# A regrouped conv result moved to every fourth partition instead of to 32 neighbouring ones

## The reference, cut to what matters

```python
# layer 0: a grouped conv, 4 groups of 16 channels, 9 taps, padding 4
out = conv(x, L0_weight, groups=4)                  # [128, 64, 1024]
x = x + out + (cond_128 @ L0_c_weight.T)[:, :, None] + fside_S_0[None, :, None]
# layers 1, 2, 3: a 1x1 conv whose 64x64 weight is mixed per sample from 8
h = gelu(gelu(cond_128 @ W0 + b0) @ W1 + b1)
att = softmax(h @ W2 + b2)                          # [128, 8]
x = x + einsum('boi,bih->boh', einsum('bk,koi->boi', att, weight), x) + (att @ bias_k)[:, :, None]
```

## Time and profile before

| what | value |
|---|---|
| median of 3 runs | 383.65 us (382.25 to 386.31) |
| span of the profiled execution, first to last instruction | 383.4 us |
| PE busy | 336.6 us, 88% of the span |
| DVE busy | 282.8 us, 74% |
| ACT busy | 242.8 us, 63% |
| POOL busy | 122.4 us, 32% |
| packets of the one DMA queue in use | 94.4% of 16 engines' span |
| TensorE clock granted, mean | 0.985 |

### The profile page before, as it was taken

One profiled execution on the slowest core, in us unless ns is written; L12 is line 12 of the kernel. 1 busy time (PEld: TensorE's weight loads), 2 busy tenths in 40 slices (PEclk: granted clock), 3 DMA queues, 4 the chain that ended last, 5 costly groups with the idle time before them and its releaser, 6 DMA issues.

```text
span 383.4 us, 6039 instructions
## 1 busy us (share of the span) xinstructions
PE 336.6 (88%) x1542; PEld 271.4 (71%) x1542; DVE 282.8 (74%) x298; ACT 242.8 (63%) x415; POOL 122.4 (32%) x172
## 2 busy tenths in 40 slices
PE   6404998799988999999999999999999999899955
PEld 5103877578867877777877887877777877777843
DVE  5711699688777877787888888877788777788463
ACT  3503597977665666666666666666666666666553
POOL 9000401234411344444444444444444311124000
PEclk9999998799999999999999999999999999999997
DMA  7896099399999999999999999999999999998985
GB/s 254 152 129 149 0 188 192 109 213 253 277 326 325 314 318 329 331 328 324 328 315 326 327 326 322 323 326 329 322 325 313 285 302 307 315 328 274 220 252 219
DMA packets 28927, 104.43 MB, mean 272 GB/s; under 512 B 3206, under 2 KB 3462, under 8 KB 20855
## 3 DMA queue, kind: packets, MB, share of 16 engines
q1 hardware_dynamic: 28919, 104.34, 94.4%
HBM read 35.89 MB, written 33.55 MB: 181 GB/s over the span
## 4 chain that ended last, share of the span: by engine, by line
PE 37%; DMA 31%; DVE 13%; issue 10%; ACT 5%; SPq 1%; DVEq 1%; ACTq 0%
PE bank L360 20%; DMA mixtab<-conv_sb 20%; DMA mixtab<-out_sb 6%; PE bank L400 5%; PE bank L402 4%; PE bank L401 4%; DMA x_sb<-in_x 4%; DVE mix_f L670 4%; DVE out_sb L684 3%; ACT conv_sb L521 2%; DVE mixtab L663 2%; PE bank L378 2%; DVE mix_lo L675 2%; DMA x_sb<-in_mats 2%; PE bank L455 1%
## 5 line engine op out<-in xcount | busy, mean ns | idle before, releaser
L521 ACT ACTIVATE conv_sb<-bank 128x512 f32<-128x512 f32 x128 | 76.5, 599 | 62.1 <-PE bank L360 58.5
L649 DVE TENSOR_TENSOR x_lo<-x_sb,x_hi 128x2064 fp32r<-128x2064 f32 x31 | 72.6, 2342 | 24.3 <-ACT x_hi L514 24.2
L360 PE MATMUL bank<-x_hi,toep_hi 128*128 128x512 f32 x256 | 86.2, 419 | 2.1 <-ACT conv_sb L521 2.1
L360 PE MATMUL bank<-x_lo,toep_hi 128*128 128x512 f32 x256 | 82.0, 402 | 0.0
L360 PE MATMUL bank<-x_hi,toep_lo 128*128 128x512 f32 x256 | 81.9, 402 | 0.0
L663 DVE TENSOR_TENSOR mixtab<-mixtab 128x2048 fp32r<-128x2048 f32 x31 | 70.7, 2281 | 0.0
L546 ACT ACTIVATE out_sb<-bank,beta 128x512 f32<-128x512 f32 x95 | 65.8, 694 | 5.5 <-PE bank L402 5.4
L400 PE MATMUL bank<-mixtab,mix_hi 128*128 128x512 f32 x128 | 54.6, 427 | 14.3 <-DVE mix_lo L675 10.6
L514 ACT ACTIVATE x_hi<-x_sb 128x2064 fp32r<-128x2064 f32 x32 | 61.6, 1924 | 2.4 <-DMA x_sb<-in_x 2.3
L658 DVE CAST mixtab<-mixtab 128x2048 fp32r<-128x2048 f32 x29 | 35.9, 1239 | 36.3 <-DMA mixtab<-conv_sb 36.0
L301 POOL COPY a_diag<-table 64x128 f32 (+1 forms) x64 | 59.3, 926 | 9.2 <-POOL a_diag L301 4.6
(11 more groups left out here) (77 smaller groups left out, 300.9 us busy)
## 6 DMA issues: line engine op xcount, KB each, us to landing
x_sb<-in_x SPq DMA_DIRECT2D x32, 1032.0 KB, 7.8
mixtab<-conv_sb SPq DMA_DIRECT2D x128, 256.0 KB, 6.3
out<-out_sb SPq DMA_DIRECT2D x31, 1024.0 KB, 8.0
out<-out_sb SPq DMA_DIRECT2D x2, 512.0 KB, 2.6
mixtab<-conv_sb SPq DMA_DIRECT2D x2, 432.0 KB
out_sb<-in_toep SPq DMA_DIRECT2D x1, 640.0 KB, 6.9
x_sb<-in_mats SPq DMA_DIRECT2D x1, 432.0 KB
mixtab<-out_sb SPq DMA_DIRECT2D x1, 432.0 KB
```

The costliest lines, as they stand in the source:

```text
L360: last = mm(o, w[:, d, g, :], v[:, par, g, :, d:d + J], start=i + d == 0, stop=i + d == 3)
L521: nc.scalar.activation(conv_sb[:, par, g, :], conv_ps[g % banks][:, :], ACT.Copy).then_inc(conv_out, 1)
L649: nc.vector.tensor_tensor(x_lo[:, par].rearrange("p g s j -> p (g s j)"), x_sb[:, par].rearrange("p g s j -> p (g s j)"), x_hi[:, par].rea ...
```

## The change

The destination of a move is every fourth partition, `g, g + 4, g + 8, ...`, instead of partitions 32g to 32g + 31. So y's partition order becomes (r, i, g) instead of (g, r, i). What multiplies y must have its rows in that order too: `a21_dup` is laid out (r, i, g), so `a21_copy` reads `pair_ps` with g as its innermost dimension, 16 elements apart, and writes without gaps; the `parity` table is reordered on the host. The number of instructions, DMAs and bytes is the same.

```diff
-        a21_dup = sb("a21_dup", [128, 2, PR, G, 2, CG])
+        a21_dup = sb("a21_dup", [128, 2, PR, 2, CG, G])
@@ move
-                sp.dma_start(y_sb[32 * g:32 * g + 32, par].rearrange("p h s j -> p h (s j)"),
+                sp.dma_start(y_sb[g::G, par].rearrange("p h s j -> p h (s j)"),
                              conv_sb[:, par, g, :]).then_inc(moved[par], 16)
@@ compose_upper
-                              a21_dup[:, par, pr].rearrange("p g r i -> p (g r i)"), a3_diag[:, par, pr, :],
+                              a21_dup[:, par, pr].rearrange("p r i g -> p (r i g)"), a3_diag[:, par, pr, :],
@@ a21_copy
-                    src = pair_ps[:, C * pr:C * pr + C].rearrange("p (g o i) -> p g o i", g=G, o=1)
-                    nc.scalar.activation(a21_dup[:, par, pr], src.to_broadcast([128, G, 2, CG]),
+                    src = pair_ps[:, C * pr:C * pr + C].rearrange("p (o g i) -> p o i g", g=G, o=1)
+                    nc.scalar.activation(a21_dup[:, par, pr], src.to_broadcast([128, 2, CG, G]),
                                          ACT.Copy).then_inc(a21_set, 1)
@@ kernel (host)
-    parity = np.zeros((G, 2, CG, 2), f)
-    parity[:, 0, :, 0] = 1
-    parity[:, 1, :, 1] = 1
+    parity = np.zeros((2, CG, G, 2), f)
+    parity[0, :, :, 0] = 1
+    parity[1, :, :, 1] = 1
```

More of the change, by code:

```diff
@@ L872 @@
         "net": pack(net, NET),
-        "kept": pack({"ident": np.eye(128, dtype=f), "parity": parity}, KEPT),
+        "kept": pack({"ident": np.eye(128, dtype=f), "parity": parity.reshape(128, 2)}, KEPT),
         "row": pack({"frow": a["fside_S_0"], "b2": np.concatenate([a[p + "b2"] for p in mixes])}, ROW),
```

## The result

The changed kernel takes 365.26 us (median of 4 runs, 364.5 to 366.36), the kernel before 384.98 us in the same session (382.25 to 388.42). The ratio is 0.953, with a 95% interval of 0.947 to 0.959: faster. The forecast was 368.0 us, with a range of 361 to 380.

A forecast was written before the change was run, and what follows sets the result against it. The prediction took the loop through the landing of a step's last move to hold steps above PE's pace; 10.8 + 2.3 + 1.0 + 1.5 = 15.6 us off 383.4, plus 0.25, gave 368.0 us, range 361 to 380.

The forecast's parts named there:

- The rate belongs to the destination: Moves: their low rate, 132 GB/s alone, comes from writing 32 neighbouring partitions; every fourth partition spans all 128.
- 390 GB/s for a spread move: Moves: rate taken for the spread destination, between bounds of 132 and 406 GB/s.
- A landing of 3.5 us: Last move of a step: lands about 3.5 us after issue instead of 5.1.
- The loop through the landing: Move, y_high, finish, mix_f, ACT, next move: closes in 9.68 us, bounds steps until the landing is under 4.7 us.
- PE is next: Steady steps: PE's own pace of 9.28 us bounds next, taken as 9.4 us with small gaps.
- The term of 10.8 us for 25 steps: Steady steps: 25 steps fall from 9.83 to 9.40 us each, saving 10.8 us, between 0 and 13.8.
- The start, 2.3 + 1.0 us: Start: ACT's 2.3 us wait for a load goes, and two early steps gain 1 us.
- The end, 1.5 us: End: the last move of step 30 lands earlier, so PE's next mix starts 1.5 us sooner, between 0 and 2.4.
- a21_copy at no cost: ACT's strided PSUM read: change of 0, at most 2 x 0.3 us a step, hidden by ACT's waits.
- (a): Rival for the moves: the rate isn't the destination's, so nothing changes, 383.5 us; chance 0.12.
- (c): Rival for the DMA engines: spread writes collide with the load, making it slower, 399 us or up to 465; chance 0.07.
- (b): Rival for steady steps: partial gain, as single landings still come late or ACT and DVE hold PE, some 376 us; chance 0.08.

The follow-up runs named there:

- e1: Kernel before with only the moves' destination spread to every fourth partition, matrix order not adapted: 366.17 us, ratio 0.951.
- e2: Changed kernel with the moves back to 32 neighbouring partitions, so only the new matrix order remains: 385.93 us, ratio 1.004 to the kernel before.
- e5: Kernel before with moves to every second partition of one 64-partition half, matrix order not adapted: 389.01 us, ratio 1.015.
- e8: Changed kernel without the third product of each mix: 356.77 us, ratio 0.931 to the kernel before.
- e10: Kernel before with ACT doing conv_copy of the last group ahead of mix_high and a finish, no DMA changed: 385.03 us, ratio 1.003.
- e13: Kernel before, moves still slow, storing only two of the four samples of a step: 369.59 us, ratio 0.961.
- e3: Kernel before with spread moves in steps 0 to 2 only, matrix order not adapted: 384.49 us, ratio 1.000.
- e4: Kernel before with spread moves from step 3 on only, matrix order not adapted: 366.87 us, ratio 0.952.
- e9: Changed kernel with the three mixing-table DMAs of the start also writing every fourth partition, result complete: 356.78 us, ratio 0.931 to the kernel before.

## Why the prediction was right, and where not

The forecast of 368.0 us was 2.7 us above the measured 365.26, and its sum of 15.6 us stands against 383.4 - 363.5 = 19.9 us between the two profiled spans.

- *The rate belongs to the destination.* Right, and shown by e1 against e2. The prediction took it that a load or a store differs from a move in just the partitions it touches; they differ in having the device memory at one end too, but e1 changes the partitions alone. The reason given, that the destination spans all 128 partitions, was too simple: by e5 a doubled span has the old rate. Which partitions it touches counts.
- *390 GB/s for a spread move.* About right: 366 GB/s in the window of 48 to 50 us of the changed kernel, and 374 and 381 in that of 50 to 52 of e1 and e8, whose packets are those of moves but for one.
- *A landing of 3.5 us.* Predicted for the last move; 3.5 us is the measured median of all moves, at a share of 0.88 where "under 0.9" was asked for.
- *The loop through the landing closes in 9.68 us and bounds the steps; it stops at 4.7 us.* This is the step of the prediction that failed. The loop is real in the chain, but with it cut (e10) the time stayed, at 1.003 of the kernel before, and the median landing grew from 5.2 to 6.3 us. What held the steps was the time that the DMA queue needs for a step's transfers, which the prediction had beside it ("from 9.8 to 7.9 us, and the queue can drain") and treated as the cause of the latency only. Its sizes for that work are estimates that e13 doesn't bear out as a plain sum. The forecast came out since both readings end at the same next bound, PE; as far as the loop goes, the right time is luck and no evidence for it.
- *PE is next, at 9.28, taken as 9.4.* Right; it was 9.31. The term of 10.8 us for 25 steps was mis-sized by the 0.09 us: from conv_copy of step 5 to that of step 30 the two profiles differ by 13.0 us.
- *The start, 2.3 + 1.0 us.* The profiles differ by 3.8 us between conv_copy of steps 0 and 5 (64.7 against 60.9), so the size fits, but the attribution doesn't. Steps 0 to 3 gave 1.7 of it and the next two 2.1. The wait of 2.3 us is absent in e2 with slow moves, and the start's gain alone is worth nothing (e3); and e4, which lacks it, stands 0.7 us from e1, less than either one's spread. It counts only where the queue doesn't take it back.
- *The end, 1.5 us.* It was 3.2 us: from the copy of step 30 to the end 27.15 us before, and 363.5 - 339.6 = 23.9 after. Of that 2.1 us lie ahead of the mix of step 31 (18.6 us before, 16.5 after), where the prediction had 2.0 at hand and counted 1.5. The other 1.1 us lie behind its start, where PE's clock was low before, told below; the prediction had no term for that.
- *a21_copy at no cost; the rest at 0.* Right: 290 ns against 297, and e2 at 1.004.
- *Rivals.* (a) and (c) fall with the result. (b) falls too, since the steps came down to 9.31 us; the late landings which it feared come back only once PE is made faster (e8).

## What to carry to other kernels

Where a DMA queue is never idle, look for the transfers whose bytes per microsecond are low with nothing beside them, and at which partitions they write: here moves to 32 neighbouring partitions passed 132 GB/s and the same moves to every fourth partition 366 to 381, for an edit of the layout alone. A chain that shows a latency loop does not prove that the loop is the bound; cut it at a cheap place and see whether the landing grows to fill the gap. Taking work out of the queue shortens the landing too, and so doesn't tell the two apart. And here what was gained before the saturated stretch was lost in it (e3), so look for the same fault first in the stretch that everything else waits for, as e9 did.

## What the runs showed of the hardware that was not expected

**POOL's copies stretch beside DVE.** In the changed kernel a_pair (L297) takes 1921 ns in the mean, where the page of the kernel before has 392. POOL's timeline, and DVE's, of the changed kernel:

```profile
212.04 2.23 POOL L297 COPY a_pair<-table 128x128 f32 x1 [4.52 <-PE bank L368]
```

```profile
211.81 2.31 DVE L649 TENSOR_TENSOR x_lo<-x_sb,x_hi 128x2064 fp32r<-128x2064 f32 x1 [1.52 <-ACT x_hi L514]
```

The copy starts 0.23 us after x_low and ends 0.15 us after it. Before, the same copy took 0.29 us at 210.83, ahead of x_low, and the copy at 211.72 (L301) was the one that took 2.22 us. The faster moves shifted the order, and another instruction pays; it costs nothing, as POOL waits 125.5 us for PE. "SBUF — State Buffer", section "Who interferes with whom", of the Trainium skill says that a DVE instruction with two SBUF inputs contends with a GpSimd instruction that reads SBUF; the timelines agree.

**PE's clock fell at both ends in the profile before, and in that of the change it did not.** Here are the windows from 62 us on, first two of the kernel before, then one of the changed kernel:

```profile
62.00:64.00 2.00, 0.82 (x8) 0.68 (x7) 1.89 (x5) 0.15 (x1) 0.18 (x1) 1.00 1.08 136
64.00:66.00 2.00, 1.75 (x7) 1.58 (x8) 1.88 (x6) 2.00 (x2) 0.00 (x0) 0.64 1.12 169
```

```profile
62.00:64.00 2.00, 0.97 (x9) 0.83 (x7) 1.89 (x5) 1.99 (x3) 0.29 (x1) 1.00 0.93 388
```

In the kernel before, PE is busy for 0.82 us of the two from 62 us on, and the granted clock is then 0.64 at 64 to 66 us and 0.51 at 66 to 68. In the changed kernel PE is busy for 0.97 us of those two, and the clock stays at 1.00 through 64 to 78 us. At the end the kernel before runs most of the last mixes at half speed, the changed kernel at full speed. The start of step 31's mix in the chain and one later piece, before and then after:

```profile
374.85 0.48 PE bank L400
...
376.19 0.43 PE bank L400
```

```profile
356.06 0.47 PE bank L400
...
358.80 0.24 PE bank L400
```

Matmuls that start every 0.43 us are those of the 1.2 GHz level, and every 0.23 to 0.24 those of 2.4 GHz. In the chain before, eight matmuls in a row have 0.41 to 0.43, 1.6 us more than at the upper level. The changed kernel's chain waits 0.9 us for a finish on ACT at that place, so that from the start of this mix to the end the two profiles differ by 1.1 us (8.55 against 7.44).

The fall doesn't belong to slow moves alone. e4, whose moves of the start are slow and where ACT waits 2.15 us for the load, shows the start's fall again (0.76 and 0.50 in the same windows). e8, whose moves are fast, has it at 66 to 70 us (0.64 and 0.51), after 0.79 us of PE work in the two before. e1, e2 and e3 don't have it at the start, though e1 has only 0.57 us of PE work at 64 to 66 us. And two of the four executions of the changed kernel have a mean clock of 0.994 and 0.995, where the profiled one has 1.000. What tips it stays open.
